# Row sums of four attention heads taken from ScalarE's exponentials instead of VectorE's reduction

## What is computed

```python
# second stage ("mixer"): convolution block, then attention, then GELU feed-forward
scores = einsum('bqhd,bkhd->bhqk', q, k) * hd ** -0.5     # hd = 16, 12 heads, 96 x 96
attn   = softmax(scores, axis=-1)
x = x + (attn @ v) @ attn_proj_w + attn_proj_b
# third stage: gated attention
q, k = layernorm(q), layernorm(k)                         # per head of 64
attn = softmax(q @ k.T * 64 ** -0.5, axis=-1)
o = gates * (attn @ v)                                    # gates by token and head, top 2 of 10 routed
out = o @ proj_w + proj_b
```

## Time and profile before

| | us |
|---|---|
| median of 3 runs | 572.84 |
| lowest, highest | 570.52, 573.50 |
| the profiled execution | 571.14 |
| its span on the core | 569.3 |

### The profile page before, as it was taken

How to read it: one execution, slowest core, us unless ns; L and a number is a source line. 1 busy time by engine, 2 the same in 40 slices (tenths; PEclk the granted TensorE clock), 3 DMA queues, 4 the chain that set the end, 5 groups by cost and what they waited for, 6 DMA issues and landing times.

```text
span 569.3 us, 11357 instructions
## 1 busy us (share of the span) xinstructions
PE 513.4 (90%) x4673; PEld 393.2 (69%) x4673; DVE 401.0 (70%) x887; ACT 304.9 (54%) x496; POOL 97.9 (17%) x85
## 2 busy tenths in 40 slices
PE   4899989968999899999999899999969799989696
PEld 3667567647886577796976576876956677686475
DVE  5134877599577948979768547879729688848982
ACT  0225436465348546857346736866445568534772
POOL 6023300100320505110010423100010231011200
PEclk9799999999999999999999999999998999999999
DMA  9994020000000000100000000000000000000000
GB/s 211 307 214 132 2 63 1 8 1 2 1 1 2 2 1 2 57 8 2 1 22 2 1 3 0 1 1 1 2 22 2 1 1 2 1 22 1 1 1 22
DMA packets 12675, 16.02 MB, mean 28 GB/s; under 512 B 6235, under 2 KB 10048, under 8 KB 12240
## 3 DMA queue, kind: packets, MB, share of 16 engines
q1 hardware_dynamic: 9712, 12.71, 8.9%
q10 hardware_dynamic: 2400, 2.00, 1.1%
q0 software_dynamic: 512, 0.59, 0.6%
HBM read 14.11 MB, written 1.18 MB: 27 GB/s over the span
## 4 chain that ended last, share of the span: by engine, by line
PE 70%; DVE 16%; ACT 7%; issue 2%; SPq 1%; DMA 1%; POOL 1%; ACTq 0%; DVEq 0%
PE ps L693 15%; PE ps L1006 10%; PE ps L703 8%; PE ps L683 7%; PE ps L826 4%; PE ps L1203 3%; PE ps L1067 3%; DVE smax L1707 3%; DVE pr L1733 2%; DVE psum L1721 2%; PE ps L1057 2%; PE ps L784 2%; PE ps L1181 2%; PE ps L841 2%; PE ps L886 2%
## 5 line engine op out<-in xcount | busy, mean ns | idle before, releaser
L1707 DVE TENSOR_REDUCE smax<-ps 96x12 f32<-96x1152 f32 (+1 forms) x28 | 37.8, 1350 | 15.3 <-PE ps L1057 10.3
L1721 DVE TENSOR_REDUCE psum<-pr 128x12 f32<-128x1152 f32 (+1 forms) x24 | 32.2, 1342 | 4.9 <-ACT pr L1374 4.9
L1369 ACT ACTIVATE pr<-ps,less 128x96 f32<-128x96 f32 (+1 forms) x96 | 24.6, 337 | 19.5 <-DVE less L1709 19.4
L1412 ACT ACTIVATE squares<-ps 128x1536 f32<-128x1536 f32 x12 | 17.4, 1451 | 26.2 <-PE ps L703 19.1
L1949 POOL TENSOR_TENSOR side_wide<-attn,w_mask 128x1024 f32<-128x1024 f32 (+1 forms) x12 | 21.6, 1824 | 56.6 <-ACT attn L1262 46.1
L1975 POOL TENSOR_TENSOR squares<-squares,qk_root 128x512 f32<-128x512 f32 x8 | 16.6, 2081 | 76.6 <-DVE qk_root L1507 76.6
L1820 DVE TENSOR_REDUCE ss<-squares 128x24 f32<-128x1536 f32 x12 | 21.0, 1748 | 10.5 <-ACT squares L1412 10.5
L1923 POOL TENSOR_TENSOR ln_root<-ln_root,minus_half 128x3 f32<-128x3 f32 x8 | 6.8, 855 | 123.7 <-DVE ln_root L1606 123.7
L683 PE MATMUL ps<-w_cqkv,side_c 64*96 64x384 f32 (+1 forms) x96 | 27.9, 503 | 0.0
L1006 PE MATMUL ps<-w_ff,b_kB 128*128 128x192 f32 x144 | 25.7, 330 | 0.0
L693 PE MATMUL ps<-w_cqkv,side_c 128*128 128x512 f32 (+1 forms) x72 | 24.9, 491 | 0.0
(11 more groups left out here) (361 smaller groups left out, 1339.4 us busy)
## 6 DMA issues: line engine op xcount, KB each, us to landing
x_in<-in_xT SPq DMA_DIRECT2D x3, 768.0 KB, 4.4
b_kB<-in_cqkv SPq DMA_DIRECT2D x1, 1152.0 KB
w_cqkv<-in_cqkv SPq DMA_DIRECT2D x1, 864.0 KB
out<-side_c ACTq DMA_DIRECT2D x3, 288.0 KB, 2.3
w_cqkv<-in_cqkv SPq DMA_DIRECT2D x1, 855.0 KB
heads<-in_xT ACTq DMA_DIRECT2D x3, 256.0 KB, 4.1
side_in<-in_patchT SPq DMA_DIRECT2D x3, 192.0 KB, 4.9
side_tok<-in_tok_ff SPq DMA_DIRECT2D x2, 288.0 KB, 6.7
```

Source lines behind the costliest of these rows:

```text
L1369: m = act.activation(e[:, s % 2, h * N:(h + 1) * N], t[0:rows, h // 4, h % 4 * N:(h % 4 + 1) * N], ACT.Exp, scale=head ** -0.5, bias=less[ ...
L1707: dve.tensor_reduce(mx, t, AX.X, ALU.max).then_inc(w.S[stage + "_sub"], 1)
L1721: dve.tensor_reduce(psum[0:rows, s % 2, :], e, AX.X, ALU.add).then_inc(w.S[done], 1)
```

## The change

With `accum_out` an ACTIVATE also adds up its results along the row and delivers the sum of each partition. The four exponentials of heads 8 to 11 now write their sums to `psum[..., 8:12]`, and VectorE's reduction covers heads 0 to 7 only: 768 columns in, 8 sums out. The reciprocal and all that follows read the same 12 sums.

```diff
@@ ScalarE, numerators
                 for h in range(DVE_LESS, NH):
                     m = act.activation(e[:, s % 2, h * N:(h + 1) * N], t[0:rows, h // 4, h % 4 * N:(h % 4 + 1) * N], ACT.Exp,
-                                       scale=head ** -0.5, bias=less[0:rows, s % 2, h - DVE_LESS:h - DVE_LESS + 1])
+                                       scale=head ** -0.5, bias=less[0:rows, s % 2, h - DVE_LESS:h - DVE_LESS + 1],
+                                       accum_out=psum[0:rows, s % 2, h:h + 1])
                 m.then_inc(w.S[stage + "_exp"], 1)
@@ VectorE, weights
                 dve.wait_ge(w.S[stage + "_exp"], w.upto(stage + "_exp", w.count(stage), 2 * s + 2))
-                dve.tensor_reduce(psum[0:rows, s % 2, :], e, AX.X, ALU.add).then_inc(w.S[done], 1)
+                dve.tensor_reduce(psum[0:rows, s % 2, 0:DVE_LESS], e[:, 0:DVE_LESS], AX.X, ALU.add).then_inc(w.S[done], 1)
```

## The result

The changed kernel takes **575.0 us** (median of 20 runs, 572.99 to 575.88) against 571.49 us for the kernel before (median of 20 runs on the same chip). The ratio is **1.0044, 95% interval 1.0033 to 1.0055**: 2.5 us slower. The medians are 3.5 us apart and the means 2.5, for the runs of both kernels lie in two groups some 2 us apart, and the median of before is in its quicker group (12 of 20 runs), that of the changed kernel in its slower one (11 of 20).

A forecast was written before the change was run, and what follows sets the result against it. TensorE, busy 90% of 569.3 us, was taken as the bound, so savings elsewhere count only in its idle time. The places summed to -0.57 us, 572.84 to 572.3 us, no measurable change; range 569.3 to 576.0 us.

The forecast's parts named there:

- walk: Place-by-place sum along TensorE's timeline, setting VectorE's savings against ScalarE's delays; total -0.57 us.
- rival 2: Dear readout not overlapped on ScalarE: TensorE waits longer at eight low-slack places; 575.7 to 579 us, chance 0.13.
- s: VectorE's saving per softmax tile from summing 768 instead of 1152 columns: 0.40 us.
- e: ScalarE's added time per softmax tile for four readouts of 0.09 us each: 0.36 us.
- rivals 1 and 2: Rival 1: the sums are free (e = 0), -3.0 us, 569.8 us, chance 0.10; rival 2 has its own line.
- 112 to 131 us: Three tiles: -0.44 at the product at 127.37 us and -0.21 at the gap at 130.94 us, together -0.65 us.
- 168 to 190 us: GELU's reader at 173.90 us +0.16, two sums on VectorE's gates that TensorE waits for -0.80; place -0.64 us.
- 297 to 321 us: GELU wait +0.36, then a single tile's exponentials +0.36 less 0.40 for its sum; place +0.32 us.
- 237, 366 and 387 us: Products behind a tile's exponentials: +0.19 each at 237 and 387 us after slack of 0.17, +0.36 at 366 us.
- 484 and 493 us: -0.40 at 484.49 us, +0.36 at 492.79 us for a copy behind a tile's exponentials; place -0.04 us.
- 500 us and the end: No term at 500 us; from 533 us, -0.40 at 541.71 us and about 0.1 back from two single tiles: -0.30.
- rival 3: TensorE's clock falls elsewhere, such as 425 to 433 us: 1 to 3 us of either sign; chance 0.14 seen alone.

The follow-up runs named there:

- Saving alone: Changed kernel without readouts: VectorE sums eight heads, the sums of heads 8 to 11 are left out (1.0 instead); 570.72 us, 0.9964 to before; again 569.67 us, 0.9973.
- first tile put back: Changed kernel with three tiles (at 112, 500 and 541 us) put back to whole sums on VectorE; 573.13 us, one execution.
- masking short: Kernel before and changed kernel, each with GpSimd's key masking in the later groups cut to 2 of 128 columns; 569.33 and 573.18 us, one execution each.
- cost alone: Changed kernel in which ScalarE delivers its four sums but VectorE still sums all twelve heads; 578.33 us, 1.0093 to the kernel before.
- chain b: Changed kernel with sums on ScalarE only in the twelve tiles of chain b, others as before; 573.12 us, 1.0008 to the kernel before.
- chains c and e: Changed kernel with sums on ScalarE only in the sixteen tiles of chains c and e; 573.59 us, 1.0024 to the kernel before.
- one group: Changed kernel with sums on ScalarE only in the four tiles of chain c's first group (234 to 267 us); 572.56 us, 1.0011 to before.
- all but this group: Changed kernel with the four tiles of chain c's first group (234 to 267 us) as before; 574.31 us, 1.0036 to the kernel before.
- four tiles: Changed kernel with sums on ScalarE only in four tiles where TensorE waits for VectorE; 570.25 us, 0.9971 to before; again 573.02 us, 1.0016.

## Why the prediction was wrong

Both prices came out as forecast, so the steps that failed are in the walk: at 121 us it took the releaser that the wait names for the only one, at 500 and 542 us it counted no cost because no wait shows, and at 190 and 321 us it let VectorE's savings through GpSimd's masking. By the traces the places come to +1.38 us instead of -0.57. That the time is inside the range all the same is owed to the room left for rival 2, a dear readout, which did not occur.

**The two prices.** s = 0.40 and e = 0.37, predicted 0.40 and 0.36. The choice between the bounds (0.056 and 0.150 a readout, 0.09 taken, 0.09 measured) was right, and rivals 1 and 2 in their first conditions, a free or a dear readout, are out.

**112 to 131 us, forecast -0.65, measured -0.27.** The step "two stand together and VectorE ... ends 2s = 0.80 earlier ... the sums start long after their exponentials, which hides e" failed. It followed VectorE alone. TensorE's wait at 121.04 is named after VectorE in the earlier trace rows, but ScalarE's copy ended only 0.12 us before VectorE did, and that copy hangs on the first tile's exponentials. Nor had the walk a term for TensorE's wait of 1.22 us at 116.21, which is for these exponentials by name: its list of waits for ScalarE begins at 127.4. So the product comes 0.34 later instead of 0.40 earlier, and the third tile's maximum, which VectorE could have started 0.80 earlier, waits 0.47 us for TensorE and comes 0.36 earlier. Its own readouts give that back at 127 us. Saving alone gives -1.01 here, and the first tile put back brings 121 us to 0.

**168 to 190 us, forecast -0.64, measured -0.20.** The GELU's +0.16 was +0.21. The -0.80 was -0.41. The second tile's multiplication ends 1.21 us behind GpSimd's first masking operation, and that one is itself held up by the first tile's multiplication and so gains one s, not two. With the masking short it is -0.60 for the place.

**297 to 321 us, forecast +0.32, measured +0.72.** The step "another 0.36 less s for its sum" failed: s was lost. The prediction had seen the overlap and left 1 us of either sign open, but put its middle at zero. In truth the sign was to be had from the trace: the masking starts behind ScalarE's copies and so 2e later, and the multiplication's end moves with the masking's, whatever s gains in front of it. With the masking short it is +0.30.

**237, 366 and 387 us, forecast +0.74, measured +0.97.** The handoffs, slack of 0.17 and all, were sized right: the products at 237 and 387 us start 0.19 to 0.20 later, as forecast, and 366 us is right to 0.01. Besides, these eight products last 2.18 us instead of 2.10, and 0.07 more comes at 243 us. Why, was not taken apart.

**484 and 493 us.** Both right to 0.01.

**500 us and the end, forecast 0 and -0.30, measured +0.28 and -0.08.** The walk counted places with a visible wait. At 498.27 TensorE has no wait in the trace of before, but the four exponentials that release its bank end at 498.05 (1.01 us from 497.04); a handoff takes 0.14 where TensorE waits for it, so the slack is 0.08. At 542.84 ScalarE's row ended 0.21 us ahead (1.01 us from 541.62). Where TensorE waits for this row, in the changed trace, it starts 0.05 us behind it (543.99 and 1.00 long, against 545.04). So the slack is 0.16, and 0.37 - 0.16 = 0.21 is what came. Neither shows as an idle time. Both are gone with one tile put back, so the term wrongly put at nothing is e less the slack, 0.29 and 0.21 us.

**The clock, rival 3.** Its price, 1 to 3 us, covers what was seen: 1.6 us at 116 us, 1.7 us at 288 us. The fall at 533 us costs nothing in the end, for the place has -0.07 with it and -0.06 in the second trace, without it. Its chance was set as if it were a rare case. In fact the falls differ between executions of one kernel: two traces of the changed kernel have them near 288, 430 and 534 us, the third at 118, 421, 430 and 518. The places give +1.4 us, and the three measurements of the changed kernel +2.5, +1.7 and +2.5. The other kernels lean the same way: cost alone +3.5 by places and +5.3 measured, saving alone -2.3 and -2.1 or -1.5, chain b +0.3 and +0.5, chains c and e +1.1 and +1.4, one group +0.3 and +0.6, all but this group +1.1 and +2.1, four tiles -1.6 and -1.7 or +0.9. That is on average 0.8 us above the places, as if the kernel before had fewer falls than its neighbours.

The clocks of the single runs say just that. Of the kernel before, 25 of the 98 runs beside the experiments have a mean granted clock of 0.988, like its profiled execution, and these are its quick ones, 571.2 to 571.6 us on average on each chip. Of the changed kernel none of 43 reaches it. Among runs at 0.985, on the same chip, the changed kernel is 1.2 us slower (573.98 against 572.83) and 1.9 us (574.43 against 572.53), about what the places give. So falls of the clock hold most of the rest by this comparison, which is not an experiment. What brings them **stays open**. Cost alone, chains c and e, and all but one group never have 0.988 either (27 runs). Chain b, one group and four tiles have it in 11 of 45, the one group in 2 of 11, for which no run at 0.988 was expected.

**The sum.** The places miss the forecast by 1.95 us. Of this 0.84 are at GpSimd's two places, and 0.82 go away with its work shortened. Another 0.88 are at the three places with a second releaser: 0.38 at 112 to 131 us, 0.28 at 500 us and 0.22 at the end. What the first tile's readouts took at 121 us, 0.34, is not the same as the 0.38 of its place. The last 0.23 are at 237 to 387 us.

## What to carry to other kernels

A wait in a trace names the last releaser. Before counting a gain there, look up when every other one ended: at 121 us, with 0.12 us between two of them, a saving of 0.4 us on one engine and a cost of 0.37 on the other came to a loss of 0.34. For a cost, search also where no wait shows, by going from each delayed instruction to its readers and comparing end and start. When two engines' operations hold each other up, find out which end hangs on which before you predict a length: here a late start of GpSimd cost VectorE in full, and an early start of VectorE gained nothing.

## What the runs showed of the hardware

- A sum delivered by an ACTIVATE is a separate instruction on ScalarE, ACTIVATION_READ_ACCUMULATOR, 0.20 us long, overlapped at both ends by about 0.1 us in the rows at 113.82 to 115.10 us. In a row of short exponentials each adds 0.09 us.
- A VectorE multiplication of 128x1152 that meets GpSimd's multiplication of 128x1024 takes up to 2.77 us instead of 1.36, and with GpSimd's operation short all are 1.36. How long it takes isn't a matter of how much overlaps. In all thirteen traces with the full masking (the one of 953 us left out), at both places, it ends 1.21 or 1.22 us behind the end of GpSimd's first operation, be it 1.41, 1.81, 2.37 or 2.77 us long. GpSimd is held up in turn: its first operation takes 1.90 us at 317.62 us in the kernel before and 2.79 at 185.22, where it meets a VectorE multiplication that runs from 184.90 to 186.26, and in the thirteen traces it ends 1.75 or 1.76 us behind the end of that one. A sum beside it isn't held up: the one at 184.61 us took 0.95 us with the masking under way since 184.42.
- In the kernel before, that one overlap at 318 us costs 1.0 us on the path: TensorE's start moved by just that with the masking short.
- The lower level of TensorE's clock appears in nearly identical stretches of work or not: from 286 to 288 us the kernel with the readouts in chains c and e has the busy times of the kernel before to 0.01 us, and its clock is at 0.66 in 288 to 290 us where before is at 1.00. First of before, then of this kernel:

```profile
286.00:288.00 2.00, 1.97 (x23) 1.95 (x24) 0.55 (x3) 1.82 (x2) 0.52 (x1) 1.00 0.45 144
```

```profile
286.00:288.00 2.00, 1.96 (x23) 1.94 (x24) 0.55 (x3) 1.83 (x2) 0.51 (x1) 1.00 0.46 145
288.00:290.00 2.00, 2.00 (x11) 1.28 (x8) 1.45 (x9) 0.25 (x1) 0.93 (x1) 0.66 0.00 0
```
